# Causal attention with output projection and layer norms: query blocks of 512 by 4 heads against query tiles of 128 by 16 heads, in one unrolled stream

## The reference

```
q = x @ wq.T + bq ; k = x @ wk.T + bk ; v = x @ wv.T + bv
scores  = q k^T / sqrt(32), -inf above the diagonal
attn    = softmax(scores) v           # per head, heads side by side
x1      = layernorm(x + attn @ wo.T + bo)
out     = layernorm(x1 + clip(x1 * sx) @ clip(w * sw) / (sx * sw))
          # sx = 448 / max|x1| over all of x1, sw = 448 / max|w|
```

## Time and profile before

| | |
|---|---|
| median of three runs | 2720.03 us |
| profiled execution | 2719.72 us, span 2718.0 us |
| mean granted clock of TensorE | 0.974 of 2.4 GHz |
| instructions | 45333 |
| busy share PE / DVE / ACT / POOL | 94% / 69% / 47% / 32% |

### The profile page before, as it was taken

The page is one execution under the profiler, slowest core; times in us unless marked ns, Lnnn a source line. Parts: engine busy times, 40 slices in busy tenths (PEclk is TensorE's granted clock), DMA queues, the critical chain, the costliest instruction groups (busy, mean ns, idle before and its releaser), DMA issues.

```text
span 2718.0 us, 45333 instructions
## 1 busy us (share of the span) xinstructions
PE 2542.1 (94%) x15400; PEld 1588.6 (58%) x15400; DVE 1879.0 (69%) x1432; ACT 1273.5 (47%) x1571; POOL 865.6 (32%) x569
## 2 busy tenths in 40 slices
PE   7999998889999999999878999999999997799998
PEld 5888885545544444444544555444444445688887
DVE  6343336668788889999555788888899993444444
ACT  2222224545566666777334565666777670100000
POOL 2321302433322222212334333222221223566663
PEclk9999998989999999999888999999999998899999
DMA  7343334411211111011233122111101104122221
GB/s 232 124 145 141 116 128 141 122 40 51 62 45 39 39 40 40 12 39 40 67 95 94 44 66 51 40 39 39 40 29 37 39 1 162 48 85 90 88 93 62
DMA packets 75076, 197.24 MB, mean 73 GB/s; under 512 B 8559, under 2 KB 8559, under 8 KB 72815
## 3 DMA queue, kind: packets, MB, share of 16 engines
q1 hardware_dynamic: 50220, 140.52, 17.9%
q10 hardware_dynamic: 24768, 55.59, 5.3%
HBM read 123.72 MB, written 72.35 MB: 72 GB/s over the span
## 4 chain that ended last, share of the span: by engine, by line
PE 62%; issue 7%; DVE 5%; ACT 5%; POOL 3%; DMA 1%; ACTq 1%; SPq 0%; DVEq 0%; POOLq 0%
PE bank L1165 16%; PE bank L1177 15%; PE bank L1153 13%; PE bank L1261 13%; ACT prob L689 4%; DVE acc L940 3%; PE bank L1195 2%; POOL prob L546 2%; PE bank L1187 2%; DMA q_st<-max_d 1%; PE bank L1250 1%; DVE acc L937 1%; POOL att_lo L538 0%; ACT att_hi L700 0%; DVE r_den L901 0%
## 5 line engine op out<-in xcount | busy, mean ns | idle before, releaser
L689 ACT ACTIVATE prob<-bank 128x1024 f32<-128x1024 f32 (+3 forms) x1280 | 1077.4, 897 | 627.6 <-PE bank L1165 595.2
L940 DVE TENSOR_TENSOR acc<-acc,prob 128x2048 f32<-128x2048 f32 (+3 forms) x512 | 1093.4, 2136 | 131.1 <-POOL prob L546 85.8
L1165 PE MATMUL bank<-q_st,keys 98*128 98x512 f32 (+3 forms) x2560 | 712.5, 392 | 88.6 <-ACT prob L689 63.0
L1165 PEld LDWEIGHTS bank<-q_st,keys 98*128 98x128 f32 x2560 | 427.6, 192 | 391.6 <-ACT prob L689 308.3
L1177 PE MATMUL bank<-prob,v_t 128*32 128x512 f32 (+3 forms) x5120 | 596.6, 548 | 11.1 <-POOL prob L546 11.1
L546 POOL TENSOR_SCALAR_AFFINE_SELECT prob<-prob 128x512 f32<-128x512 f32 x256 | 300.8, 1179 | 873.0 <-ACT prob L689 872.4
L1075 PE MATMUL bank<-xt_hi,w_hi 128*128 128x512 f32 x576 | 227.3, 395 | 16.4 <-DVE xt_lo L777 15.7
L1075 PE MATMUL bank<-xt_hi,w_lo 128*128 128x512 f32 x576 | 226.6, 393 | 0.0
L1075 PE MATMUL bank<-xt_lo,w_hi 128*128 128x512 f32 x576 | 226.2, 393 | 0.0
L1177 PEld LDWEIGHTS bank<-prob,v_t 128*32 128x32 f32 x5120 | 107.9, 109 | 197.8 <-issue 141.4
L1261 PE MATMUL bank<-wf_hi,xs_hi 128*128 128x512 f32 x512 | 202.8, 396 | 0.0
(11 more groups left out here) (118 smaller groups left out, 2668.7 us busy)
## 6 DMA issues: line engine op xcount, KB each, us to landing
q_st<-q_hi_d SPq DMA_DIRECT2D x128, 256.0 KB
xt_raw<-x_t SPq DMA_DIRECT2D x16, 1024.0 KB, 6.9
q_hi_d<-part_hi ACTq DMA_DIRECT2D x64, 256.0 KB, 2.1
q_lo_d<-part_lo ACTq DMA_DIRECT2D x64, 256.0 KB, 2.3
q_st<-q_lo_d SPq DMA_DIRECT2D x64, 256.0 KB
x<-x_d SPq DMA_DIRECT2D x32, 512.0 KB, 3.2
out<-y ACTq DMA_DIRECT2D x32, 512.0 KB, 2.6
res<-x SPq DMA_DIRECT2D x24, 512.0 KB, 4.0
```

Of the source, the lines that this page charges most:

```text
L689: nc.scalar.activation(prob[:, t % SLOTS, 2 * p:2 * p + 2, off:NB], bank[:, 2 * p:2 * p + 2, off:NB], ACT.Exp, scale=SCALE).then_inc(p_don ...
L940: nc.vector.tensor_tensor(acc[:, r, :, off:NB], acc[:, r, :, off:NB], new, ALU.add).then_inc(acc_done, 1)
L1165: last = nc.tensor.matmul(bank[:, h, off:NB], keys[:, b * JB + t // QT, t % QT * P:(t % QT + 1) * P], q_st[:, slot, h, off:NB], start=True ...
```

## The change

- A group is now one tile of 128 queries with half of the heads (16). Its scores are still four products of 512 columns, four heads at 128 queries each. Tile i needs i+1 key tiles, and every step is full. The diagonal key tile is taken first (t = 0), the others follow in order; only step 0 of a group is masked, by two `affine_select`s of two banks each.
- Tiles are taken in pairs (15-k, k), 34 steps a pair, and their groups in turn: long, short, long, short (the last pair: long, long, short, short). 64 groups, 544 steps, both batches in one stream without a boundary.
- All engines run the stream unrolled, `for s in range(STEPS + SLOTS_OVER)`. `places(q)` gives, for each tile, the steps of its parts, relative to the pair after its own: SPLIT, HALF0, HALF0_END, SUM0, HALF1, HALF1_END, SUM1, SCALE_ROW, LARGEST.
- The bias goes into the projection as one more product per half: `share` (all 2/128) times `bo_parts`, whose lower 64 rows hold bo's upper part and whose others the rest. POOL's addition goes.
- The normalisation moves from DVE to ACT (`Identity` with scale and bias); POOL computes the bias -mean/deviation in a third small operation, `shift_of`.
- Queries have three buffers, loaded two groups ahead, in runs of 128 columns (512 bytes) where there were 512. `res` and `x1_sent` are doubled, `piece` has its own buffer, the `end_*` buffers go.
- PE starts only after `share` is set, which waits for wo's last cut.

```diff
+        PAIR = 2 * (TT + 1)
+        pairs = [(b, k) for b in range(B) for k in range(TT // 2)]
+        tiles = [(b, i) for b, k in pairs for i in (TT - 1 - k, k)]
+        groups = []
+        for p in range(len(pairs)):
+            a, c = 2 * p, 2 * p + 1
+            if p < len(pairs) - 1:
+                groups += [(a, 0), (c, 0), (a, 1), (c, 1)]
+            else:
+                groups += [(a, 0), (a, 1), (c, 0), (c, 1)]
...
+        den_at = []
+        for n in range(len(groups)):
+            at = begins[n] + lengths[n] + 1
+            den_at.append(max(at, den_at[-1] + 4) if n else at)
...
+        def places(q):
+            p, second = divmod(q, 2)
+            if p < len(pairs) - 2:
+                names = (21, 24, 29, 30, 32, 37, 38, 40, 42) if second else (4, 7, 12, 13, 15, 20, 21, 23, 25)
+                base = (p + 1) * PAIR
+            elif p == len(pairs) - 2:
+                names = (17, 20, 23, 24, 26, 29, 30, 32, 33) if second else (4, 7, 10, 11, 13, 16, 17, 19, 20)
+                base = (p + 1) * PAIR
+            else:
+                names = (39, 40, 40, 41, 40, 40, 41, 42, 43) if second else (30, 33, 34, 35, 36, 37, 38, 39, 40)
+                base = p * PAIR
+            return [base + at for at in names]
...
+            def shift_of(moments, done, before):
+                wait_apart(pool, done, before + (NH + 3))
+                nc.gpsimd.tensor_scalar(moments[:, 3:4], moments[:, 0:1], moments[:, 2:3], -1.0, ALU.mult, ALU.mult).then_inc(done, 1)
@@ block.gpsimd @@
+            for s in range(STEPS + SLOTS_OVER):
+                if s < STEPS and steps[s][1] == 0:
+                    for p in range(2):
+                        pool.wait_ge(p_done, 2 * s + p + 3)
+                        tri = prob[:, s % SLOTS, 2 * p:2 * p + 2].rearrange("p g (a n) -> p (g a) n", n=P)
+                        nc.gpsimd.affine_select(out=tri, in_=tri, compare_op=ALU.is_ge, fill=0.0, base=0,
+                                                pattern=[[0, 2 * HG], [1, P]], channel_multiplier=-1).then_inc(masked, 1)
+                if s in split_at:
...
+                    nc.gpsimd.tensor_tensor(att_lo[:], att[:, q % TILES_KEPT], att_hi[:].bitcast(F32), ALU.subtract).then_inc(att_cut, 1)
+                if s in sum1_at:
+                    q = sum1_at[s]
+                    inverse_deviation(moments[:, q % 2], ln1, q * LN)
+                    shift_of(moments[:, q % 2], ln1, q * LN)
@@ block.scalar @@
+            for s in range(STEPS + SLOTS_OVER):
+                if s < STEPS:
+                    act.wait_ge(pv_done, s + 1)
+                    act.wait_ge(acc_done, s + 1)
+                    for p in range(2):
+                        act.wait_ge(s_done, 2 * s + p + 2)
+                        nc.scalar.activation(prob[:, s % SLOTS, 2 * p:2 * p + 2], bank[:, 2 * p:2 * p + 2], ACT.Exp, scale=SCALE).then_inc(p_done, 1)
...
+                if s in split_at:
+                    q = split_at[s]
+                    act.wait_ge(att_ready, last_group[q] + 3)
+                    act.wait_ge(y_done, 2 * q)
+                    nc.scalar.activation(att_hi[:], att[:, q % TILES_KEPT], ACT.Copy).then_inc(att_hi_cut, 1)
+                if s in scale_at:
+                    q = scale_at[s]
+                    act.wait_ge(ln1, q * LN + LN - 2)
+                    nc.scalar.activation(res[:, q % 2], res[:, q % 2], ACT.Identity, bias=moments[:, q % 2, 3:4], scale=moments[:, q % 2, 2:3]).then_inc(ln1, 1)
@@ block.tensor @@
+            for s in range(-1, STEPS + SLOTS_OVER):
+                if s + 1 < STEPS:
+                    scores(s + 1)
+                if 1 <= s <= STEPS:
+                    weigh_values(s - 1)
+                if s in group_of_den:
+                    denominators(group_of_den[s])
+                if s - 3 in group_of_den:
+                    spread_out(group_of_den[s - 3])
+                for q, half, part, parts in fillers.get(s, []):
+                    half_projection(q, half, part, parts)
```

More of the change, by code:

```diff
@@ L276, in stored_alone @@
[L276 to L294, removed]
@@ new lines, in build @@
+        for p in range(len(pairs)):
[4 more added lines that the diff above has]
+                groups += [(a, 0), (a, 1), (c, 0), (c, 1)]
+        lengths = [tiles[q][1] + 1 for q, u in groups]
+        begins = [sum(lengths[:n]) for n in range(len(groups))]
+        steps = [(n, t) for n in range(len(groups)) for t in range(lengths[n])]
+        STEPS = len(steps)
+        SLOTS_OVER = 14
@@ new lines, in at_place @@
+        def at_place(name):
+            return {places(q)[name]: q for q in range(TILES)}
+        SPLIT, HALF0, HALF0_END, SUM0, HALF1, HALF1_END, SUM1, SCALE_ROW, LARGEST = range(9)
+        split_at, sum0_at, sum1_at = at_place(SPLIT), at_place(SUM0), at_place(SUM1)
+        scale_at, largest_at = at_place(SCALE_ROW), at_place(LARGEST)
+        fillers = {}
+        for q in range(TILES):
+            at = places(q)
+            for half, first, last in ((0, at[HALF0], at[HALF0_END]), (1, at[HALF1], at[HALF1_END])):
+                for place in range(first, last + 1):
+                    fillers.setdefault(place, []).append((q, half, place - first, last - first + 1))
@@ L306, in wait_apart, with tile_row, key_tile, attended @@
+        PIECE_EVERY, PIECE_CLIP = 6, 4
+        def tile_row(q):
+            return tiles[q][0] * TT + tiles[q][1]
+        def key_tile(s):
+            n, t = steps[s]
+            b, i = tiles[groups[n][0]]
+            return b * TT + (i if t == 0 else t - 1)
+        def attended(n):
+            q, u = groups[n]
+            return flat(att[:, q % TILES_KEPT, u * HG:(u + 1) * HG])
+        def y_bank(q, half):
+            return DEN_BANK if q == TILES - 1 and half == 1 else Y_BANK
         def wait_apart(eng, semaphore, value):
@@ L723, in _ @@
+            act.wait_ge(y_done, 2 * TILES)
             for k in range(KT):
@@ new lines, in scores @@
+            def scores(s):
+                n, t = steps[s]
+                if t == 0:
+                    pe.wait_ge(q_in[n % 3], 64 * (n // 3 + 1))
+                queries = q_st[n % 3].rearrange("p (a g) n -> p a g n", g=HG)
+                k = key_tile(s)
+                for p in range(2):
+                    pe.wait_ge(p_done, 2 * s + p + 1)
+                    for g in (2 * p, 2 * p + 1):
+                        last = nc.tensor.matmul(bank[:, g].rearrange("p (a n) -> p a n", n=P), keys[:, k // QT, k % QT * P:(k % QT + 1) * P], queries[:, :, g], start=True, stop=True)
+                    last.then_inc(s_done, 1)
@@ new lines, in weigh_values @@
+            def weigh_values(s):
+                n, t = steps[s]
+                if t == 0:
+                    pe.wait_ge(pv_moved, n + 1)
+                    pe.wait_ge(masked, 2 * n + 2)
+                pe.wait_ge(p_done, 2 * s + 4)
+                k = key_tile(s)
+                for g in range(HG):
+                    last = nc.tensor.matmul(bank[g * HD:(g + 1) * HD, 4 + n % 2], v_t[:, k // QT, k % QT], prob[:, s % SLOTS, g],
+                                            start=(t == 0), stop=(t == lengths[n] - 1), skip_group_check=True)
+                last.then_inc(pv_done, 1)
```

496 lines of the change are left out of this document (173 added, 323 removed).

## The result

The changed kernel takes 2797.9 us (median of 4 runs, 2793.8 to 2800.5); beside it on the same chips the kernel before takes 2718.3 (2715.8 to 2721.1). The ratio is 1.029, with a 95% interval of 1.027 to 1.031. The forecast was 2814.

A forecast was written before the change was run, and what follows sets the result against it. PE's work was taken to bound the stream: 2719.7 - 146 = 2574 us, plus 174 for ScalarE's wait and 66 for the clock, gave 2814 us; the range was 2605 to 2860.

The forecast's parts named there:

- Parts 1 to 5: Stream: full steps 1153, projection 368, denominators 125, work beyond PE's 28 + 16, ends 14.5; 1705 against 1851 us.
- The bias: Projection on PE: one more product per half, 64 x 0.23 = 15 us.
- Part 5: Ends of the batches: the boundary goes, 24.5 us dropped; 14.5 us of waits stay at the very end.
- Part 6: Scaling in ScalarE's queue: waits for POOL's operations, blocked by VectorE's additions; mean 5.8 us in 30 tiles, 174 us.
- Part 7: PE's pauses at each scaling wait: clock falls to half, about 2.2 us each, 30 x 2.2 = 66 us.
- the clock stays up: Rival, at PE's pauses: the wait comes but the clock does not fall; 2748 us, chance 0.15.
- the query loads: Loads of 512-byte pieces, four times as many, issued 17 steps ahead: nothing taken; without that lead up to 15 us a group.
- The masks of double size: Rival, at group starts: masks hold up value products, 65 us more, about 2880 us, chance 0.10.
- the unrolled stream: All engines' step loop: nothing taken for 28 loop turns; any gain at most PE's idle time.
- POOL is not held up: Rival, after a tile's statistics: POOL's operations run undisturbed, a tile costs 1.4 to 2 us; 2622 us, chance 0.30.

The follow-up runs named there:

- the early loads: On top of the scaling six steps behind, the last phase's first loads issued inside the stream, ahead of the last tile's store: 2559.5 us, ratio 0.941.
- the filled kernel: Changed kernel plus twenty products whose result nobody reads where PE pauses, in 30 places: 2756.3 us, ratio 1.014.
- the six-step kernel: Changed kernel with ScalarE's scaling six steps behind a tile's statistics instead of two (one tile near the end four): 2568.7 us, and 2567.8 once more.
- the kernel in which VectorE yields: Changed kernel with VectorE waiting behind a tile's statistics until POOL's three small operations are done: 2665.3 us, ratio 0.980.

## Why the prediction was right

- **Parts 1 to 5, the stream without waits.** 2574 was the sum, 2568 the measurement, and this is closer than its parts deserve. It left out the last phase's first loads, which stand behind the last store: 8 us, as the early loads showed. So the other terms were together some 14 us too large. A pair of 34 steps takes 103.2 us without the waits (872.96 to 976.18; 105 in the text) and 120.8 with them (909.04 to 1029.86; 120). The bias was sized at 0.23 us per product and measured 0.29. The boundary between the batches went as Part 5 says.
- **Part 6, ScalarE's wait.** The mechanism came as written: the first two operations blocked by additions 22 and 23, the third free. From the end of exponential 21 (907.28) the moments took 12.0 us in a tile where the normalisation stands ahead of the sum (the prediction: 10.1 and one more), but exponential 23 ended at 6.05 (913.33) and not at 5.5. So the stop in front of the scaling has the predicted length: 4.6 us, or 5.6 in five of eight pairs, is 5.2 on average, and 5.2 was measured. Wait and scaling together cost 188 us by the filled kernel, some 180 by the estimate there, against 174. Two of its terms were small: the scaling takes 1.24 us and not the 1.03 assumed from an exponential (30 x 0.2 = 6 us), and exponential 24 was to start 0.55 us behind 23 without the scaling, a figure for which the prediction shows no row; in the tile of the six-step kernel it starts 0.17 us behind.
- **Part 7, the clock.** It fell as foreseen, in the tile shown within 3 us of the last value product, and cost 42 us by the filling, some 50 by the estimate, against 66. The term that was mis-sized is "half clock for 4 to 5 us of work costs about 2.2 us: 30 x 2.2". In the tile shown there are 6.6 us of work at half clock, and they cost 2.6 us, not half of 6.6: with the clock up, the first two steps behind the scaling go at ScalarE's pace (four exponentials in 3.85 us without a gap). And not every tile pays that; in the 20 us around the scaling, half clock lasts 3.6 to 10.4 us in 29 of the 30 tiles and does not come in one. Parts 6 and 7 together were to cost 240 us and cost 230. They err in opposite directions (6 to 14 us too little and 16 to 24 too much), so that the closeness of this sum is in part luck.
- **A row misread in Part 7.** "A pause of 3.1 us near the end of batch 2 left it at 1.00" holds only to the end of the window that was read, 2247. The next microsecond of the kernel before:

```profile
2247.00:2248.00 1.00, 0.00 (x0) 0.00 (x0) 1.00 (x2) 0.00 (x0) 0.00 (x0) 0.69 0.89 356
```

The clock falls at 2247.4 there, 1.8 us after PE had gone back to work (2245.6) and 0.7 us into its next pause. It was the argument for the rival that the clock stays up, and it was none.
- **The rest.** Taking nothing for the query loads held: the packets doubled (75076 to 150742), and in the pair of the six-step kernel no piece of the chain is a load. The masks of double size took 1.27 us on average and PE's value products waited for none. Neither was changed by itself, nor was the unrolled stream run against a looped one; a few us may lie in each, and no run says which of the terms of Parts 1 to 5 were the 14 us too large.
- **The rivals.** "POOL is not held up" did not come in the kernel after. Nearest to it is the kernel in which VectorE yields; there a tile costs (2665.3 - 2568.3) / 30 = 3.2 us and not 1.6, of which the clock is 22 / 30 = 0.7. "The clock stays up" was to give 2748; the kernel that keeps it up in all but five tiles by filling the pause gives 2756.

## What to carry to other kernels

Before an operation moves to another engine, look at what stands behind it in that engine's queue, and at who makes its input: the scaling is one us of work, and what it cost was every exponential queued behind a result that was 5.5 us away. If such a result must be waited for, put the waiting instruction as many steps later as the slowest path of its input needs (here six; four were too few, five were not tried), or on the engine whose own work causes the delay. Chains of tiny operations on GpSimd beside back-to-back additions of two inputs should be priced in additions, up to one for each operation. And when a clock is read behind a pause, the window must reach beyond the point where the engine has gone back to work.

## What the runs showed of the hardware that was not expected

- The clock fell behind one pause of 2.60 us and not behind another of 2.58 in the same place, and it fell 2.2 us *after* PE had gone back to work. In the filled kernel it fell at 851.7, 1.6 us after PE was back from a pause of only 1.64 us, and behind a pause of the same length one tile later it did not. Eight unused products in the pauses of 2.6 us were worth 22 us, twenty in the long ones 42 us. The Trainium skill (TensorE: Matmul & The Clock Gate, What's actually happening) says that the observation runs freely, without regard to the kernel's own timing; two equal pauses with different outcomes are what that would give. No run here was made to test it.
- A blocked GpSimd operation ended right at the end of the running addition even when VectorE had the next one ready: L519 ended at 916.07, and between it and L521 there were 0.18 us in which addition 23 began. In the tiles shown, the moment between two additions was enough for one operation and not for the next, which has to wait for the addition behind it.
- An activation with a scale and a bias from SBUF over 128x1024 takes 1.24 us, a copy of the same size into float32r 1.06 (L712), and the same scaling on VectorE 0.81.
